# Eight gather buffers and an eight-entry loop body in the first layer of a graph network on one Trainium2 core

## The reference, cut to what matters

```
z2 = concatenate([node_feat[src], node_feat[dst], edge_feat])   # per edge
e = relu(z2 @ W_pre + b_pre)
s = segment_sum(e, dst);  q = segment_sum(e * e, dst)
mx = segment_max(e, dst); mn = segment_min(e, dst)
```

## Time and profile before

| | |
|---|---|
| median of 3 runs | 7348.3 us (7335.72 to 7362.3) |
| profiled execution, span | 7200.7 us |
| median less span | 147.6 us |
| busy in the span | PE 74%, DVE 56%, POOL 53%, ACT 42% |
| edge stage of the first layer, first to last `d2` | 110.8 to 3077.5 us, 404 entries |

### The profile page before, as it was taken

The page is one execution under the profiler, slowest core; times in us unless marked ns, Lnnn a source line. Parts: engine busy times, 40 slices in busy tenths (PEclk is TensorE's granted clock), DMA queues, the critical chain, the costliest instruction groups (busy, mean ns, idle before and its releaser), DMA issues. The chain is left out here.

```text
span 7200.7 us, 135903 instructions
## 1 busy us (share of the span) xinstructions
PE 5306.6 (74%) x31642; PEld 4026.1 (56%) x31642; DVE 4043.0 (56%) x12632; ACT 2988.5 (42%) x8170; POOL 3792.6 (53%) x3867
## 2 busy tenths in 40 slices
PE   4777777777777777785888786677777777777774
PEld 3555555555555555543666664566666666566664
DVE  5656656665666666665555555455455555455557
ACT  2444444444444444423666664233333333333335
POOL 3555555555555555502555551666666666666662
PEclk7888888888888888896888886555555555555555
DMA  5433333433334333332111111222222222222222
GB/s 158 106 99 101 100 99 99 102 103 99 101 102 105 100 99 103 100 95 57 39 39 38 38 39 26 44 44 43 44 43 44 44 44 44 44 43 44 43 44 46
DMA packets 531406, 504.25 MB, mean 70 GB/s; under 512 B 328647, under 2 KB 390672, under 8 KB 531023
## 3 DMA queue, kind: packets, MB, share of 16 engines
q0 software_dynamic: 122832, 255.14, 15.7%
q1 hardware_dynamic: 337654, 130.31, 8.6%
q10 hardware_dynamic: 70794, 117.58, 4.9%
HBM read 476.98 MB, written 25.63 MB: 70 GB/s over the span
## 5 line engine op out<-in xcount | busy, mean ns | idle before, releaser
L604 POOL DMA_INDIRECT G<-Atab,ms x1616 | 1577.2, 976 | 1411.2 <-DVE EE L627 523.5
L1840 POOL DMA_INDIRECT Gt<-TAB,metat x1632 | 1606.2, 984 | 1067.2 <-issue 454.6
L1304 POOL DMA_INDIRECT Gc<-XS,metac x560 | 542.1, 968 | 500.9 <-PE Sc L1495 233.4
L2010 PE MATMUL SR<-P,Gt 128*128 128x64 f32 x3264 | 803.8, 428 | 0.0
L701 ACT COPY BS<-BK 128x512 f32<-128x512 f32 x808 | 436.2, 588 | 872.0 <-remote 855.7
L2010 PEld LDWEIGHTS SR<-P,Gt 128*128 128x128 f32 x3264 | 727.1, 328 | 47.8
L1882 DVE TENSOR_REDUCE lt<-MT 128x1 f32<-128x256 f32 x408 | 170.2, 417 | 978.1 <-DMA WB<-Btab 958.2
L662 DVE TENSOR_TENSOR acc<-acc,TT 128x64 f32 (+1 forms) x808 | 178.4, 233 | 862.8 <-remote 534.9
L1998 PE MATMUL PT<-ident,EX 128*128 128x128 f32 x816 | 269.5, 434 | 520.3 <-ACT EX L1960 481.9
L805 PE MATMUL SX<-BS,oh 128*32 128x256 f32 x3232 | 564.7, 475 | 69.6 <-issue 47.3
L754 PE MATMUL SS<-EE,oh 128*32 128x256 f32 x3232 | 571.5, 465 | 48.4 <-issue 46.8
(11 more groups left out here) (288 smaller groups left out, 10615.3 us busy)
## 6 DMA issues: line engine op xcount, KB each, us to landing
mm<-MM ACTq DMA_DIRECT2D x202, 512.0 KB
ZR<-in_eft SPq DMA_DIRECT2D x202, 256.0 KB
Gt<-TAB,metat POOLq DMA_INDIRECT x1632
tb<-DF SPq DMA_DIRECT2D x202, 128.0 KB
G<-Atab,ms POOLq DMA_INDIRECT x1616
dq<-DQ SPq DMA_DIRECT2D x12, 768.0 KB, 5.9
Gc<-XS,metac POOLq DMA_INDIRECT x560
ad<-ADT SPq DMA_DIRECT2D x408, 0.5 KB
```

What stands on the lines that cost most here:

```text
L604: e.indirect_dma_start(G[:, k, s, :], None, Atab, bass.IndirectOffsetOnAxis(ap=ms[:, k, s:s + 1], axis=0)).then_inc(l_g[k], 16)
L1304: e.indirect_dma_start(G[:, k, s, :], None, XS, bass.IndirectOffsetOnAxis(ap=meta[:, k, s:s + 1], axis=0)).then_inc(l_g[k], 16)
L1840: e.indirect_dma_start(G[:, k, s, :], None, TAB, bass.IndirectOffsetOnAxis(ap=meta[:, k, s:s + 1], axis=0)).then_inc(l_g[k], 16)
L2010: m = e.matmul(SR[q][:, 0:2 * W], G[:, k, s, 0:128], P[:, q, s * 2 * W:(s + 1) * 2 * W], start=(s == 0), stop=(s == 3))
```

## The change

The row numbers and the gathers get eight slots in place of four. The load of `ms` becomes an SP function of its own, `load_src`, at lag 0; the other SP loads of a pair come at lag 4, and `load_dst` at lag 6. `d2` writes its sum back into the slot of `G`; `a1` reads it there. `EE`, which now holds only relu and square, has two slots, and `a1` waits in addition for `p2` of the entry two back. The gather waits for the relu of the entry eight back (`s_r`). The loop body becomes eight entries, and `T` is rounded to a multiple of eight: from 404 to 408.

```diff
-                for k, m in ((0, 2), (1, 3)):
+                for k, m in ((0, 3), (1, 3)):
...
-        ms = sbt(ph, "ms", [128, 4, 4], I32)
+        ms = sbt(ph, "ms", [128, 8, 4], I32)
...
-        G = sbt(ph, "G", [128, 4, 4, 128])
-        EE = sbt(ph, "EE", [128, 4, 2, CH])
+        G = sbt(ph, "G", [128, 8, 4, 128])
+        EE = sbt(ph, "EE", [128, 2, 2, CH])
...
-        U, D = 4, 8
+        U, D = 8, 8
...
+            def load_src(j):
+                if j.o % 2:
+                    return
+                k = j.slot(8)
+                c = keep(e, regs, j, pair_of(e, tb, j))
+                if not j.first(8):
+                    wait_sync(e, l_g[k], 64 * j.uses(8, -1), s_sync)
+                    wait_sync(e, l_g[k + 1], 64 * j.uses(8, -1), s_sync)
+                e.dma_start(ms[:, k:k + 2, :], d["meta"][ds(c, 2), :, 0:4].rearrange("a p s -> p a s")).then_inc(l_ms[k // 2], 16)
...
-                c = keep(e, regs, j, pair_of(e, tb, j))
+                c = e.snap(regs[j.slot(8)], min_val=0, max_val=NCH - 2)
...
-                if not j.first(4):
-                    wait_sync(e, l_g[k], 64 * j.uses(4, -1), s_sync)
-                    wait_sync(e, l_g[k + 1], 64 * j.uses(4, -1), s_sync)
-                e.dma_start(ms[:, two, :], d["meta"][ds(c, 2), :, 0:4].rearrange("a p s -> p a s")).then_inc(l_ms[r], 16)
...
-            pipeline(e, T, U, D, [(0, loads), (2, load_dst)])
+            pipeline(e, T, U, D, [(0, load_src), (4, loads), (6, load_dst)])
...
-                k = j.slot(4)
-                wait_pair(e, l_ms, j, 16)
-                if not j.first(4):
-                    wait(e, s_d2, j.at(-3))
+                k = j.slot(8)
+                if j.o % 2 == 0:
+                    e.wait_ge(l_ms[k // 2], 16 * j.uses(8))
+                if not j.first(8):
+                    wait(e, s_r, j.at(-7))
...
-                wait(e, l_g[j.slot(4)], 64 * j.uses(4))
-                e.tensor_tensor(EE[:, j.slot(4), 1, :], Z[:, :],
-                                G[:, j.slot(4), :, :].rearrange("p s f -> p (s f)"), ALU.add).then_inc(s_d2, 1)
+                wait(e, l_g[j.slot(8)], 64 * j.uses(8))
+                g = G[:, j.slot(8), :, :].rearrange("p s f -> p (s f)")
+                e.tensor_tensor(g, Z[:, :], g, ALU.add).then_inc(s_d2, 1)
...
-                q = j.slot(4)
+                q = j.slot(2)
                 wait(e, s_d2, j.at(1))
-                e.activation(EE[:, q, 0, :], EE[:, q, 1, :], ACT.Relu).then_inc(s_r, 1)
+                if not j.first(2):
+                    wait(e, s_p2, j.at(-1))
+                e.activation(EE[:, q, 0, :], G[:, j.slot(8), :, :].rearrange("p s f -> p (s f)"), ACT.Relu).then_inc(s_r, 1)
...
-                if j.o >= -2:
+                if j.i is T and j.o >= -2:
```

More of the change, by code:

```diff
@@ L519, in phase_l0 @@
         l_we = sem("l_we")
-        l_ms = [sem(f"l_ms{k}") for k in range(2)]
+        l_ms = [sem(f"l_ms{k}") for k in range(4)]
         l_md = [sem(f"l_md{k}") for k in range(2)]
@@ L524, in phase_l0 @@
         l_m = [sem(f"l_m{k}") for k in range(2)]
-        l_g = [v["sem"](f"l_g{k}") for k in range(4)]
+        l_g = [v["sem"](f"l_g{k}") for k in range(8)]
         s_zr = sem("l_zr")
@@ L555, in _ @@
             T = load_T(e, tb, 0)
-            regs = [e.alloc_register(f"l_chunk{k}") for k in range(4)]
+            regs = [e.alloc_register(f"l_chunk{k}") for k in range(8)]
+            def load_src(j):
[7 more added lines that the diff above has]
+                e.dma_start(ms[:, k:k + 2, :], d["meta"][ds(c, 2), :, 0:4].rearrange("a p s -> p a s")).then_inc(l_ms[k // 2], 16)
             def loads(j):
@@ L585, in load_dst @@
                 k = j.slot(4)
-                c = e.snap(regs[k], min_val=0, max_val=NCH - 2)
+                c = e.snap(regs[j.slot(8)], min_val=0, max_val=NCH - 2)
                 if not j.first(4):
@@ L748, in p2 @@
                 for s in range(4):
-                    mm = e.transpose(ET[q][:, s * 128:(s + 1) * 128], EE[:, k, 0, s * 128:(s + 1) * 128], ident[:, :])
+                    mm = e.transpose(ET[q][:, s * 128:(s + 1) * 128], EE[:, q, 0, s * 128:(s + 1) * 128], ident[:, :])
                 mm.then_inc(s_p2t, 1)
@@ L753, in p2 @@
                     r = 2 * q + s % 2
-                    mm = e.matmul(SS[r * W:(r + 1) * W, 0:256], oh[:, k, s, :], EE[:, k, :, s * 128:(s + 1) * 128],
+                    mm = e.matmul(SS[r * W:(r + 1) * W, 0:256], oh[:, k, s, :], EE[:, q, :, s * 128:(s + 1) * 128],
                                   start=(s < 2), stop=(s >= 2))
```

## The result

| in the same set of runs | before | after |
|---|---|---|
| median | 7352.89 us (7335.72 to 7362.3, 4 runs) | 7414.98 us (7407.38 to 7418.79, 4 runs) |
| profiled execution; its span | - | 7418.79 us; 7417.0 us |

The ratio is 1.0081, with an interval of [1.0062, 1.01]: 62 us slower. That lies inside the range of the prediction and inside the range of its likeliest case (7325 to 7425), 41 us above the predicted 7374. The chances had put nearly the same weight on faster (0.43) and slower (0.42).

A forecast was written before the change was run, and what follows sets the result against it. The prediction took the ring of PE and DVE, with PE disturbed during long gather runs, to bound the edge stage. Terms +29 + 7 - 10 = +26 us on 7348.3 gave 7374 us, range 6960 to 7480.

The forecast's parts named there:

- likeliest case: Edge stage: the pace stays at 7.36 us per entry; 7374 us in all, own range 7325 to 7425; chance 0.42.
- Four more entries in the edge stage, +29: Edge stage: T goes from 404 to 408, 4 x 7.36 = +29 us at an unchanged pace.
- Eight slots, 0: Edge stage: gathers come some 52 us early in place of 23, worth 0 since d2 does not wait for them.
- The start, +7: Start of the edge stage: POOL issues 16 more gathers without a pause, at 11 us per entry; +7 us.
- Row numbers ahead, 0: SP loads: ms comes 4 entries earlier, POOL's 210 us of waits for it go but lie in slack; 0.
- Sum into the gather slot and two slots of `EE`, 0: DVE and ACT: same DVE operation; a1's wait for p2 is about 0.1 us, covered by ACT's idle time; 0.
- Body of eight, -10: Edge-stage loop: 50 back-edges in place of 99 on each engine; between 0 and 31 us less, taken as -10.
- Around the span, 147.6 us: Whole kernel: the median lies 147.6 us above the profiled execution's span, carried over unchanged into the forecast.
- First rival: Edge stage: single releases break gather runs after four, PE keeps its rate; pace 6.7, -239, 7109 us; chance 0.38.
- Second rival: Edge stage: POOL runs of twelve or more gathers stall PE; pace 7.73, +181, 7529 us; chance 0.15.
- Third: Edge stage: the longer loop body no longer fits, exposing instruction fetches; +96 us, 7470 us; chance 0.05.
- The stall itself: Edge stage: long runs of gathers go with a slow PE; 14.5 us per pair worked out, 14.7 measured.

The follow-up runs named there:

- e4: Kernel after with only one, two or three gathers per entry: 6202.31, 6250.52 and 6779.56 us; 0.8463, 0.8516 and 0.9416 of the kernel before.
- e5: Kernel before with only the entries rounded to a multiple of eight (408): 7393.86 us beside 7345.61, ratio 1.007.
- e6: Kernel after with POOL held to four entries ahead, so half of its eight slots are in use: 7404.9 us beside 7345.61 for the kernel before, 1.0089.
- e1_before: Kernel before, unchanged, run again for a second profile: 7334.42 us beside 7338.72, ratio 1.0005.
- e3: Kernel after with a 0.97 us POOL memset once per entry behind the four gathers: 7304.04 us beside 7338.72 for the kernel before, 0.9952.
- e7: Kernel before with a POOL memset of 0.98 us after each entry's gathers: 7238.43 us beside 7345.61, ratio 0.9864.
- e10: Kernel before with a 0.55 us POOL memset behind every gather, so gathers are issued 1.65 us apart: 6935.33 us beside 7203.46, ratio 0.963.
- e8: Kernel after with a quarter of the bytes per gathered row: 7309.23 us beside 7197.74 for the kernel before, ratio 1.0152.
- e9: Kernel after with mask loads of 128 columns in place of 1024 per pair: 7305.04 us beside 7197.74 for the kernel before, ratio 1.0146.

## Why the prediction was right, point by point

The range was wide, 6960 to 7480 us, and the forecast of +26 us met a result of +62. The likeliest case was the right one, an unchanged pace. The half of the cost that it missed lies in the convolution.

- **What bounds the stage.** Right: the ring of PE and DVE, disturbed, with the gathers far ahead. e4 shows the ring at 4.64 us when the gathers are thinned out.
- **Four more entries in the edge stage, +29.** Right; e5 shows +34.8 in two single executions.
- **The missed term.** "Each goes through every function of every engine" was taken for the edge stage only. The convolution walks the end of the same list, 576 gathers in place of 560, and 4 x 7.4 = 30 us were missing. The count of its gathers (x560, four for each of 140 entries, the line L1304) in the profile of before could have told it. This term is the distance between the forecast and the result.
- **Eight slots, 0.** Right in the steady state, as far as single executions can tell (e6). **The start, +7.** Mis-sized: 20 us from first to eighth `d2`, since PE nearly stands still under 25 gathers on end, worse than the 11 us per entry read from the earlier trace rows.
- **Row numbers ahead, 0.** The wait for `ms` went and POOL's idle time did not: it was slack.
- **Sum into the gather slot and two slots of `EE`, 0.** The value holds, the 0.1 us that it was reasoned from do not. Relu waits for `d2` and `p2` alone, and DVE's signals are prompt, so both the 67.7 us of "PE SS" and the 234.7 us of "remote" in front of L688 are the wait for `p2`: 302 / 265 = 1.1 us per entry. It is covered: in `e1_before` ACT idles 1.67 us per entry in front of relu and 2.33 in front of the copies, after the change 2.48 and 1.47, 4.0 us together both times. After and e5, which lacks both edits, agree within their intervals.
- **Body of eight, -10.** Not visible: it lies below the spread of single executions.
- **Around the span, 147.6 us.** Wrong as a reading (1.8 us lie there), harmless in the sum, since it stood in for the difference between a quick and a slow execution. But the pace of 7.36 us belonged to the quicker one; the four entries cost 7.65 each in the runs that decide.
- **First rival (pace improves, 0.38).** Single releases from relu do not break up POOL's gathers, they only make the pattern four and eight in place of the earlier one. And it would not have been enough: with every run broken up after four PE does not keep its good rate (e3, 7.38 us; e7, 7.34). The rival was priced at a pace of 6.7 us; e10 reached just that, by spreading out the four themselves.
- **Second rival (runs of twelve, 0.15).** None of the 301 runs past 300 us in the trace after is longer than eight. **Third (fetches, 0.05).** No packets in the stage.
- **The stall itself.** The prediction read "long runs of gathers" from the earlier trace rows, by counting PE's records. That reading was at best a part of it, and that its sum of 14.5 us per pair fitted was luck: runs of four are enough (e3, e7), and PE's signals are late from the second gather on, while its records still come at the good rate. It did no harm to the forecast, which left the pace as it was. Shown is that the spacing within the four matters (e10), that one or two gathers per entry do next to no harm (e4), and that the bytes of the gathers and of the masks do not matter (e8, e9). Why is open.

## What to carry to other kernels

Before a buffer is doubled, find the instruction that waits for its contents; if there is none, look at what the producer does to the others while it runs ahead. A count that is rounded up for one loop is rounded up for every loop that walks the same list, so price it in each. An engine that is ahead can be slowed down at no cost up to the point where it becomes the bound, and a pause in the right place may be the cheapest edit there is: 0.55 us behind each gather gave 3.7% here. When an engine waits for a record that ended long before, look at the signal and not only at the records.

## What the runs showed of the hardware

- Beside indirect gathers of 128 rows issued 1.26 us apart, TensorE's semaphore signals reach the other engines 2.3 us after the end of its records on average and up to 8.8 us (after); with one gather per entry it is 0.04 us, with four of them 1.65 us apart 0.07. The signals of the other engines are 0.01 us behind in all of these.
- In the same stretches gaps open between TensorE's records that no wait explains: eight records of `p4` in 3.5 us in place of 1.06. With the gathers 1.65 us apart the stage runs at POOL's own rate.
- The loss does not grow evenly with the number of gathers: 4.64, 4.75, 6.21 and 7.62 us per entry with one to four of them (three of them on a quicker chip).
- The same kernel took 7198 and 7203 us on two chips and 7339 and 7346 us on two others, 2% apart, more than twice the effect of this change.
- Instruction packets in a loop rose from 59 to 103 in 855 us by a change elsewhere in the program, and the loop took the same time.
